# A two-layer transformer kernel: the second routing's norm, turns and router logits move into the attention's output stage

## The reference

```
x = x + 0.5 * L0_ffn(layernorm(x))      # mixture of 8 experts, top 2: first routing
x = x + L0_attn(layernorm(x))           # 16 heads, one K and V; its last step is out @ o_w.T
x = x + 0.5 * L0_ffn(layernorm(x))      # the same experts again: second routing
x = x + 0.5 * L1_ffn(...); x = x + L1_attn(...); x = x + 0.5 * L1_ffn(...)
```

```
logits = (y * rsqrt(mean(y*y) + 1e-6) / sqrt(512) * router_scale) @ router_logits   # [4096, 8]
choices = top 2 of 8 per token; weights = softmax shares of the two
out = sum of the two experts' gelu(gate) * up @ linear, by those weights
```

## Time and profile before

| | us |
|---|---|
| median of 3 runs (4774.04 to 4779.06) | 4774.67 |
| the profiled execution | 4780.76 |
| its span | 4779.2 |
| PE busy in the span | 4579.4 |
| DVE busy | 2885.2 |
| output stage, first matmul to last add | 2538.99 to 2629.98 |
| second routing, first DMA issue to last DVE instruction | 2632.96 to 2745.59 |

### The profile page before, as it was taken

How to read it: one execution, slowest core, us unless ns; L and a number is a source line. 1 busy time by engine, 2 the same in 40 slices (tenths; PEclk the granted TensorE clock), 3 DMA queues, 4 the chain that set the end, 5 groups by cost and what they waited for, 6 DMA issues and landing times. The chain is left out here.

```text
span 4779.2 us, 82403 instructions
## 1 busy us (share of the span) xinstructions
PE 4579.4 (96%) x27966; PEld 3492.0 (73%) x27967; DVE 2885.2 (60%) x5285; ACT 2108.4 (44%) x4111; POOL 2255.8 (47%) x1724
## 2 busy tenths in 40 slices
PE   6999996999999999999999699999899999999999
PEld 4888885666666666666667488888788877778888
DVE  6222225789999999999974733322455548754444
ACT  4222224467666676766762422222322235533222
POOL 0545434178888888888881054543111007500000
PEclk8999998899999999999999799999899999999999
DMA  7232326657777777777765734433522112250110
GB/s 220 87 104 93 104 78 235 238 111 147 146 147 146 146 146 146 146 149 150 148 135 154 223 108 136 130 124 108 177 67 71 58 49 82 71 198 27 36 36 27
DMA packets 246003, 585.98 MB, mean 123 GB/s; under 512 B 30816, under 2 KB 85088, under 8 KB 221152
## 3 DMA queue, kind: packets, MB, share of 16 engines
q0 software_dynamic: 62064, 317.23, 29.5%
q1 hardware_dynamic: 183536, 263.86, 16.7%
HBM read 263.27 MB, written 121.63 MB: 81 GB/s over the span
## 5 line engine op out<-in xcount | busy, mean ns | idle before, releaser
L1401 POOL TENSOR_TENSOR attend_pairs<-attend_pt 128x1024 f32<-128x1024 f32 x512 | 1257.5, 2471 | 200.4 <-ACT attend_pt L1366 199.7
L1414 DVE TENSOR_REDUCE attend_mx<-attend_am_ps 128x1 f32<-128x512 f32 x2048 | 1252.0, 679 | 125.0 <-PE attend_am_ps L1274 121.8
L1366 ACT ACTIVATE attend_pt<-attend_sc_ps 128x512 f32<-128x512 f32 x2048 | 1040.3, 617 | 286.0 <-PE attend_sc_ps L1262 285.9
L1274 PE MATMUL attend_am_ps<-attention_kst,attend_qst 96*128 96x512 f32 x2048 | 859.4, 425 | 10.2 <-DMA attend_qst<-q_parts 10.1
L1262 PE MATMUL attend_sc_ps<-attend_qst,attention_kst 98*128 98x512 f32 x2048 | 816.6, 400 | 1.5 <-ACT attend_pt L1366 1.3
L1665 PE MATMUL ffn_gu_ps<-ffn_y_hi,ffn_w 128*128 128x512 f32 (+1 forms) x1584 | 566.6, 367 | 3.1 <-DVE ffn_y_lo L1795 3.0
L1274 PEld LDWEIGHTS attend_am_ps<-attention_kst,attend_qst 96*128 96x128 f32 x2048 | 393.2, 192 | 241.1 <-DVE attend_mx L1414 123.5
L1665 PE MATMUL ffn_gu_ps<-ffn_y_lo,ffn_w 128*128 128x512 f32 (+1 forms) x1584 | 566.0, 366 | 0.0
L759 DVE TENSOR_TENSOR expert_ac<-expert_gu_ps,expert_gl 128x512 f32<-128x512 f32 x142 | 98.2, 692 | 747.6 <-ACT expert_gl L706 710.3
L1288 PE MATMUL attend_pv_ps<-attend_pt,attention_v 128*32 128x256 f32 x8192 | 495.1, 382 | 0.0
L1262 PEld LDWEIGHTS attend_sc_ps<-attend_qst,attention_kst 98*128 98x128 f32 x2048 | 389.9, 191 | 87.1 <-ACT attend_pt L1366 11.7
(11 more groups left out here) (329 smaller groups left out, 7472.8 us busy)
## 6 DMA issues: line engine op xcount, KB each, us to landing
attend_pairs<-attend_pairs POOLq DMA_DIRECT2D x189, 1024.0 KB
weights_raw<-experts_dram POOLq DMA_DIRECT2D x76, 512.0 KB
ys<-expert_ob SPq DMA_DIRECT2D x142, 256.0 KB
attend_qst<-q_parts SPq DMA_DIRECT2D x192, 128.0 KB, 4.0
yn<-route_yb SPq DMA_DIRECT2D x64, 256.0 KB
ffn_xb<-x SPq DMA_DIRECT2D x64, 256.0 KB, 2.9
keyvalue_xb<-x SPq DMA_DIRECT2D x64, 256.0 KB, 2.7
weights_lo<-experts_dram SPq DMA_DIRECT2D x24, 512.0 KB
```

Source lines behind the costliest of these rows:

```text
L1274: pe.matmul(am[:, bank, :], qst[0:KROWS, n % 2, h * HALF + hd, :], kst[0:KROWS, o:o + 4 * P], start=True, stop=True).then_inc(am_rdy, 1)
L1366: act.activation(pt[:, u % RING, g * 4 * P:(g + 1) * 4 * P], sc[:, s % SBANKS, :], ACT.Exp, scale=HD ** -0.5).then_inc(p_rdy, 1)
L1401: pool.tensor_tensor(pairs[:, slot(half, j), :], pt[:, 2 * p % RING, :], pt[:, (2 * p + 1) % RING, :], ALU.add).then_inc(pair_rdy, 1)
L1414: dve.tensor_reduce(mx[:, hh, block:block + 1], am[:, am_slot["max", a] % MBANKS, :], AX.X, ALU.max).then_inc(mx_rdy, 1)
```

## The change

The output stage now does the second routing's work per tile. Its DVE adds the residual into one of four `ob` buffers, takes statistics of it in SBUF, normalises the tile before and stores it through SP to `yn`; PE turns the tile two behind and makes the logits of the tile three behind, with the turned tile `yT` as the stationary operand and the 8 router columns as the moving one, so that they come out by tokens and need neither `lgT` nor the 32 small transposes. The product with `rr` ends the stage and leaves the SBUF tile `logits`. The loops of the output stage are written out (no `Fori`). The second `routing_stage` gets `given=logits` and leaves out its tile loop, its loads of x and of the router's weights; its DVE waits for the expert scales (`w_in`, 16) and two of the POOL constants, and for the other constants only ahead of `hot(0)`. The first routing keeps its code, but for this last wait. The core of the diff:

```diff
-def routing_stage(nc, stage, const, x, scale, logits_w, expert_scale, w_experts, box, yn, plan):
+def routing_stage(nc, stage, const, x, scale, logits_w, expert_scale, w_experts, box, yn, plan, given=None):
...
+            if given:
+                dve.wait_ge(w_in, 16)
+                dve.wait_ge(iotas, 2)
+                lg = given
+            else:
+                router()
...
-def output_stage(nc, stage, const, attn, w_hi, w_lo, x, x_new):
+def output_stage(nc, stage, const, attn, w_hi, w_lo, x, x_new, scale, logits_w, yn, logits_out):
...
+            for t in range(NT):
+                sp.wait_ge(o_rdy, t + 1)
+                sp.dma_start(x_new[t * P:(t + 1) * P, :], ob[:, t % NX, :]).then_inc(x_st[t % NX], 16)
+                if t + NX < NT:
+                    load(t + NX)
+                if t:
+                    keep(t - 1)
...
+            high(0)
+            high(1)
+            for t in range(NT):
+                if t + 2 < NT:
+                    high(t + 2)
+                if t >= 2:
+                    turned(t - 2)
+                deviation(t)
+            turned(NT - 2)
+            turned(NT - 1)
...
+            for t in range(NT):
+                add(t)
+                if t:
+                    scale_of(t - 1)
+                dve.wait_ge(o_rdy, t + 1)
+                dve.bn_stats(bn[:, t % 2, :], ob[:, t % NX, :]).then_inc(bn_rdy, 1)
+                if t:
+                    normalise(t - 1)
+                dve.wait_ge(bn_rdy, t + 1)
+                dve.bn_aggr(mv[:, t, :], bn[:, t % 2, :]).then_inc(mv_rdy, 1)
+                if t + 2 < NT:
+                    low(t + 2)
...
+            def logits(t):
+                if t == 0:
+                    pe.wait_ge(wr_rdy, DC)
+                pe.wait_ge(yT_rdy, t + 1)
+                for c in range(DC):
+                    ins = pe.matmul(lg[:, t, :], yT[:, t % 2, c * P:(c + 1) * P], wr[:, c, :],
+                                    start=(c == 0), stop=(c == DC - 1), skip_group_check=True)
+                ins.then_inc(lg_rdy, 1)
+            for t in range(NT):
+                out(t)
+                if t >= 3:
+                    logits(t - 3)
+                if t >= 2:
+                    turn(t - 2)
+            logits(NT - 3)
+            turn(NT - 2)
+            turn(NT - 1)
+            logits(NT - 2)
+            logits(NT - 1)
```

More of the change, by code:

```diff
@@ L193, in load @@
                 sp.dma_start(xb[:, k, :], x[bass.ds(t * P, P), :]).then_inc(x_in[k], 16)
[L195 to L199, removed]
+            if not given:
+                for t in range(NX):
+                    load(t, t)
+                    sp.sem_inc(y_st[t], 16)
+                sp.dma_start(wl[:], logits_w).then_inc(w_in, 16)
+                sp.dma_start(rs[:], scale).then_inc(w_in, 16)
             sp.dma_start(esc[:], expert_scale.partition_broadcast(P)).then_inc(w_in, 16)
@@ L206, in step @@
                 sp.dma_start(yn[bass.ds(t * P, P), :], yb[:, k, :]).then_inc(y_st[k], 16)
[L208 removed]
+            if not given:
+                looped(sp, NT, NX, step)
             for n in range(2 * WPIECES):
@@ L270, in keep @@
                 act.activation(lgT[0:E, bass.ds(t, 1), :], lgT_ps[k].unsqueeze(1), ACT.Copy).then_inc(lgT_kept, 1)
[L272 to L276, removed]
+            if not given:
+                deviation(0, 0)
+                looped(act, NT, NX, step, head=True)
+                keep(NT - 1, (NT - 1) % 2)
+                act.wait_ge(step_done, 3)
+                act.activation(small["msd"][:], small["ms"][:], ACT.Sqrt).then_inc(msd_rdy, 1)
             act.wait_ge(gap_rdy, 1)
@@ L311, in step @@
                     turn(t + 2, k + 2)
[L313 to L317, removed]
+            if not given:
+                pe.sem_inc(yT_rdy, 4)
+                pe.sem_inc(lgT_kept, 2)
+                pe.wait_ge(wr_rdy, DC)
+                turn(0, 0)
+                turn(1, 1)
+                looped(pe, NT, NX, step)
+                pe.wait_ge(lgT_kept, NT + 2)
+                for t in range(NT):
+                    ins = pe.transpose(lg_ps[:, t, :], lgT[0:E, t, :], const["ident"][0:E, 0:E])
+                ins.then_inc(lg_rdy, 1)
             pe.wait_ge(both_rdy, 1)
@@ L1492, in _, with load @@
[L1492 to L1505, removed]
+            def load(t):
+                sp.dma_start(xb[:, t % NX, :], x[t * P:(t + 1) * P, :]).then_inc(x_in[t % NX], 16)
@@ L1507, in _, with high @@
+            keep(NT - 1)
+            for k in range(NX):
+                sp.wait_ge(x_st[k], 16 * (NT // NX))
+                sp.wait_ge(y_st[k], 16 * (NT // NX))
         @block.scalar
         def _(act):
-            act.sem_inc(pr_rdy, 2)
-            def step(t, k, i, last):
-                act.wait_ge(pr_rdy, t + 1)
-                act.activation(a_hi[:, k % 2, :].unsqueeze(1), rows(t), ACT.Copy).then_inc(hi_rdy, 1)
-            looped(act, NT, NX, step)
+            def high(t):
+                if t >= 2:
+                    act.wait_ge(pr_rdy, t - 1)
+                act.activation(a_hi[:, t % 2, :].unsqueeze(1), rows(t), ACT.Copy).then_inc(hi_rdy, 1)
@@ new lines, in _ @@
+            low(0)
+            low(1)
+            dve.wait_ge(w_in, 32)
+            for c in range(DC):
+                dve.tensor_scalar(wr[:, c, :], wl[:, c, :], rs[:, c:c + 1], float(D) ** -0.5, ALU.mult, ALU.mult).then_inc(wr_rdy, 1)
+            for t in range(NT):
[10 more added lines that the diff above has]
+                    low(t + 2)
```

158 lines of the change are left out of this document (107 added, 51 removed).

## The result

The change makes the kernel faster: 4751.44 us, median of 5 runs (4751.20 to 4754.40), where five runs of the kernel before, the three shown above among them, have 4779.06. The ratio over all these runs is 0.9948 [0.9933, 0.9963], so 24.9 us less (17.7 to 32.0); the two medians differ by 27.6, inside that range. 29.9 were forecast.

The account below looks back on a forecast made before the run. PE was taken to bound the output stage. Removing 78.0 us, less 37.7 added on PE and 10.4 of tail, gives 29.9 off the 4774.67 median: 4744.8 us, with 8 in 10 between 4733 and 4754.

Parts of the forecast that it names:

- What bounds the stage: Output stage: PE sets the pace, 4.05 us a tile without idle time, and DVE's add is released by PE.
- Added on PE: Output stage: transposes and logits add 1.33 us a tile to 2.72, 37.7 us ahead of the last product's end.
- the key-value row: Profile row from the key-value stage, like-shaped logits and transposes between large matmuls: 1.40 us, or 1.26 summed from parts.
- The two bounds: Limits on PE's added work per tile: 1.56 us from the routing's own loop, 0.98 using the 8-row transposes.
- Hidden on DVE and ACT: Output stage: DVE's 2.94 us a tile, some 3.1 with waits, fits under PE's 4.05, a cover of 0.9.
- Moved, the tail: Serial hand-overs after the output stage's last product: `best` starts 10.4 us behind it, ±2.
- The close with the scales' transfer: End of the tail: the close costs 1.15 us, then DVE waits for the expert scales, 2.91 from issue to release.
- Shifted, the weights: Experts' weights issued 3.3 us later against the DVE chain, covered by 5.6 us of slack: cost nothing.
- PE doing less: Rival, chance 0.14: logit weight loads in the output stage cost 0.067 a record, 27.9 us for 37.7, time 4735.
- DVE as the bound: Rival, chance 0.13: DVE or the ring between engines stretches the output stage's tile to, say, 4.5 us, time 4762.
- The weights' chain: Rival, chance 0.04: the experts' weights arrive too late behind the routing, price 1 to 4 us, up to 4749.
- The low clock: Rival, chance 0.03: PE falls to 1.2 GHz in the output stage, tiles take twice 4.05 us, time 4858.

Follow-up runs that it names:

- scale_early: Changed kernel with the expert scales loaded in the output stage, so `best` waits for no transfer: 4745.65 us, ratio 0.9929 to the kernel before.
- columns_moved: Changed kernel with logits in the old form (8 router columns stationary, 128 tokens moving, copies, 32 small transposes), still in the output stage: 4764.27 us, ratio 0.9960.
- stats_thrice: Changed kernel with DVE taking each tile's statistics three times, the extra results unused: 4754.39 us, ratio 0.9953 to the kernel before.
- warm_tail: Changed kernel with unused 128-column matmuls ahead of the last logits, meant to keep the clock up: 4756.9 us, ratio 0.9950 to the kernel before.
- tokens_only: Kernel before with logits by tokens in both routings' own loops, nothing moved into the output stage: 4809.15 us, ratio 1.0063.
- again: The changed kernel unedited, run once more beside the kernel before: 4752.06 us, ratio 0.9945.
- both_mended: Changed kernel with both tail repairs, expert scales loaded in the output stage and spare matmuls ahead of the last logits: 4749.78 us, ratio 0.9932.
- one_chunk: Changed kernel making only the first of each tile's four logit matmuls, so the choice of experts changes: 4731.17 us, ratio 0.9899.
- stats_five: Changed kernel with DVE taking each tile's statistics five times, four results unused: 4779.74 us, ratio 0.9996 to the kernel before.
- tokens_warm: Kernel before with logits by tokens in both routings' own loops, plus four unused 128-column records per tile: 4871.15 us, ratio 1.0188.

## Why the prediction was right, and where it was off

**What bounds the stage:** right. PE has no gap in it, and DVE's idle time ahead of the add is released by PE.

**Added on PE:** right to 0.2 us in 38. The tile is 4.06 for 4.05, the logits 0.81 and the turn with its slower follower 0.48 for 0.85 and 0.48. Some of this closeness is luck: what was added came to 1.29 (the key-value row by its parts had 1.26, the middle taken was 1.33), and 0.05 a tile, which no term of the prediction held, came on top in the large matmuls. In scale_early it is missing, and the tile is 4.02. The row that fitted stands between large matmuls, as the new code does. The two bounds, a register loop and 8-row transposes, were both far off. By the figure of the Trainium skill ("TensorE: Matmul & The Clock Gate", section "LDWEIGHTS (loading the stationary operand)") the prediction's estimate for the eight loads was 0.85, and this trace is near it (0.81 for the eight records). What the prediction drew from that page, an argument against logits by tokens, did not hold here: with 8 columns loaded and 128 moving, columns_moved measured 0.97 and a slower step ahead.

**Hidden on DVE and ACT:** right, with a cover of 1.5 in place of 0.9. The prediction added up durations (2.94, with waits 3.1). But instructions of 0.69 us start 0.61 apart (2599.67 and 2600.28 in stats_thrice, as 2655.16 and 2655.77 above), so the tile is 2.53.

**Moved, the tail:** the mechanism right, the size off, and this is the step that failed: 10.4 ± 2 was forecast, 12.9 and 12.5 came. Up to the product it counted 6.0 us, with the last turns and logits at the full clock; 8.2 and 7.8 were measured, at the lower level from some 3 us behind the last add on. With the clock held up (warm_tail) it is 6.2: nearly the whole miss is the clock. The prediction asked about the clock for the tiles only, and set it aside because the routing's loop, with transposes and small matmuls, ran at 0.93. That row has 128 moving columns in its logits; with 8 in their place tokens_only ran at 0.50, so it did not bear on the new form. The close with the scales' transfer was counted 4.06 (1.15 and 2.91), with 0.42 for the product 4.5, and is 4.7: SP's issue came 0.3 sooner and the transfer took 0.5 longer (3.43). So the tail took 2.5 us more than forecast and the stage 0.2 more, and 29.9 became 27.2.

**Shifted, the weights:** right. They went out 3.0 us ahead of `best` in place of 5.8, and had landed by 2708 all the same. The chain behind `best` stays at 38.0 in again and at 38.1 in scale_early and both_mended.

**The rest of the difference** need not be of the change. By the ratio 24.9 (17.7 to 32.0), in again 26.3 (20.1 to 33.0): both hold 27.2, and the 28.2 of the wider marks. The measured 4751.44 is 6.6 above the forecast 4744.8, and 4.4 of that is the base: the forecast took the median of three runs, and two more put it at 4779.06. A single profile carries some microseconds of its own from stages that nothing touches.

**The rivals:** PE doing less is ruled out by one_chunk. DVE as the bound is real and begins 1.5 us away, by stats_thrice and stats_five. The weights' chain did not appear. The low clock is absent from the tiles, costs 1.6 us in the tail, and is there all through the loop when the same logit form stands in the two routings, which then take 30 us more. (The chance of "faster", given as 0.94, is 0.93 by the prediction's own terms.)

## What to carry to other kernels

Work per tile that stands in a loop of its own in which no engine is full can be worth hiding in a neighbour that one engine fills, even at PE's full price: here 37.9 us paid, 65.1 saved. Price it by a row that stands in the same surroundings, and count the tail apart, as a serial list of hand-overs with the clock and the first transfer behind the close in it. When an operand order is turned round, try it where it will stand: the same by-tokens logits are the cheaper form between large matmuls and 30 us dearer in the routings' own loops.

## What the runs showed of the hardware

- Fp32 matmuls of 8 moving columns with 128 x 128 weights start 0.10 us apart per record at full clock (0.81 for eight, between large matmuls) and 0.20 at half (1.57 for eight, tokens_only). 128 moving columns with 8 columns of weights take 0.12 per record (0.97 for eight, columns_moved), the dearer form at full clock.
- In a loop of only such matmuls and transposes the granted clock stays at 0.50 though PE is busy 60.0 of 60 us; the 128-moving form in the same loop has 0.93 with PE less busy. Four records more of 128 columns per tile did not change it (0.50 in tokens_warm).
- In the output stage's tail, with turns and by-tokens logits alone behind the last large matmul, the clock fell to 0.50. With the old form's matmuls there it did not, though PE paused as long (0.69 us): the last 16 records of columns_moved took 1.92 us; in warm_tail, with spare matmuls of 128 columns, the 16 of the new form took 1.95.
